# Moving two of VectorE's per-step products to GpSimd, and keeping the output chain in PSUM, in a scan kernel for eight cores

## The reference, cut to what matters

```python
xn = layernorm(x)
x_in, res = silu(xn @ Win[:D].T), xn @ Win[D:].T
dlt, B, C = split(x_in @ Wx.T)                      # 16, 1024 and 1024 wide
delta = clip(softplus(dlt @ Wdt.T + b), 1e-5, 0.1)
# for each token t, each of 1024 channels, each of 16 states:
dA = clip(exp(A * delta), 1e-6, 1)
h  = clip(h * dA + B * delta * x_in, -100, 100)
y  = sum(h over states) * C + Dp * x_in
out = x + (y * silu(res)) @ Wout.T + b_out + ffn(xn)
```

## Time and profile before

| | |
|---|---|
| time, median of 3 runs | 1364.24 us (1362.29 to 1365.52) |
| the profiled execution | 1363.85 us |
| its span on the slowest core (core 5) | 1362.3 us |
| DVE busy | 1329.3 us, 98% |
| ACT busy | 1190.7 us, 87% |
| PE busy | 1159.2 us, 85% |
| POOL busy | 72.0 us, 5% |

### The profile page before, as it was taken

How to read it: one execution, slowest core, us unless ns; L and a number is a source line. 1 busy time by engine, 2 the same in 40 slices (tenths; PEclk the granted TensorE clock), 3 DMA queues, 4 the chain that set the end, 5 groups by cost and what they waited for, 6 DMA issues and landing times.

```text
span 1362.3 us, 16727 instructions; the slowest of 8 cores (1356.8 to 1362.3 us)
## 1 busy us (share of the span) xinstructions
PE 1159.2 (85%) x4352; PEld 454.8 (33%) x4352; DVE 1329.3 (98%) x821; ACT 1190.7 (87%) x1899; POOL 72.0 (5%) x101
## 2 busy tenths in 40 slices
PE   5687886899888888799997898898888999878987
PEld 2232332333333333233333343333333333333432
DVE  6899999999999999999999999999999999999996
ACT  3899989989899898998989989899988988799781
POOL 1010100000000000000000000000000000110100
PEclk9886776878778898777778887788977888898877
DMA  9666855455654465444583555554554346454421
GB/s 278 100 110 98 126 99 141 108 109 89 117 117 72 109 124 98 104 111 86 117 127 72 102 116 126 80 108 92 106 101 90 54 78 139 82 147 85 93 50 63
DMA packets 94508, 143.97 MB, mean 106 GB/s; under 512 B 31232, under 2 KB 55360, under 8 KB 94416
## 3 DMA queue, kind: packets, MB, share of 16 engines
q1 hardware_dynamic: 80736, 117.99, 35.4%
q0 software_dynamic: 13680, 24.91, 17.4%
HBM read 101.45 MB, written 35.65 MB: 101 GB/s over the span
## 4 chain that ended last, share of the span: by engine, by line
PE 28%; DVE 28%; issue 21%; ACT 18%; DMA 4%; DVEq 1%; ACTq 0%; SPq 0%
DVE h L734 24%; ACT da L894 10%; PE pS L500 7%; PE pB L467 4%; DMA u<-u 3%; PE pC L477 3%; PE pX L435 2%; PE pO L435 2%; PE pR L487 2%; PE pO L514 2%; PE pO L511 2%; PE pX L511 2%; DVE y L750 1%; PE pX L514 1%; ACT L894 1%
## 5 line engine op out<-in xcount | busy, mean ns | idle before, releaser
L734 DVE TENSOR_TENSOR_SCAN h<-da,u 128x2056 f16<-128x2056 f16 x256 | 1119.5, 4424 | 3.4 <-ACT da L877 1.8
L894 ACT ACTIVATE da<-dl,consb 128x512 f16<-128x512 f16 x1024 | 651.7, 711 | 1.7 <-DVE dl L753 1.0
L500 PE MATMUL pS<-h,eye 128*128 128x512 f16 x1024 | 316.5, 442 | 160.3 <-DVE h L734 160.1
L500 PEld LDWEIGHTS pS<-h,eye 128*128 128x128 f16 x1024 | 102.2, 107 | 340.5 <-issue 316.0
L467 PE MATMUL pB<-xin,wx 128*128 128x512 f16 x512 | 167.9, 488 | 2.8 <-DMA wx<-w_x 2.2
L477 PE MATMUL pC<-xin,wx 128*128 128x512 f16 x512 | 140.8, 425 | 0.0
L487 PE MATMUL pR<-xnT,win 128*128 128x512 f16 x512 | 137.0, 417 | 0.0
L365 POOL DMA_DIRECT2D yt<-ost x56 | 47.8, 854 | 1049.1 <-ACT ost L955 1017.2
L467 PEld LDWEIGHTS pB<-xin,wx 128*128 128x128 f16 x512 | 54.3, 116 | 96.1 <-issue 87.2
L477 PEld LDWEIGHTS pC<-xin,wx 128*128 128x128 f16 x512 | 55.6, 109 | 79.1 <-issue 63.3
L894 ACT ACT_TABLE_LOAD x63 | 80.8, 1283 | 1.1
(11 more groups left out here) (140 smaller groups left out, 917.6 us busy)
## 6 DMA issues: line engine op xcount, KB each, us to landing
wo<-wos SPq DMA_DIRECT2D x56, 512.0 KB, 6.5
xt<-x SPq DMA_DIRECT2D x48, 512.0 KB, 5.9
u<-u SPq DMA_DIRECT2D x62, 384.0 KB, 3.2
yt<-xt SPq DMA_DIRECT2D x60, 256.0 KB, 7.8
yt<-ost POOLq DMA_DIRECT2D x56, 256.0 KB, 5.6
wx<-w_x POOLq DMA_DIRECT2D x15, 256.0 KB, 8.9
xnT<-x SPq DMA_DIRECT2D x4, 512.0 KB, 7.1
da<-w_in SPq DMA_DIRECT2D x4, 512.0 KB, 11.3
```

The lines of the kernel that those rows point to most:

```text
L500: mm = te.matmul(pS[s % 2][:, :], eye[:, :], h[:, n * SEG + 2:(n + 1) * SEG], start=(n == 0), stop=(n == NST - 1))
L734: v.tensor_tensor_scan(h[:, g * GW:(g + 1) * GW], da[:, g * GW:(g + 1) * GW], u[p][:, :], 0.0, op0=ALU.mult, op1=ALU.add).then_inc(v_scan, 1)
L894: sc.activation(da[:, n * SEG + 2:(n + 1) * SEG], dl[s % 2][:, :], AF.Exp, scale=cc(C_AL + k * NST + n)).then_inc(act_da, 1)
```

## The change

`t1` and `u` of steps 2 to 63 are computed on GpSimd, in a new function `dt_x(w)` that heads GpSimd's part of step s = w−1. It waits until DVE has finished scan(s,0). DVE keeps them only for steps 0 and 1. The tile `y1` goes: the three output operations work in place in the PSUM bank `pS[z % 2]` and follow one another on DVE with nothing between. clip_carry of groups 1 to 3 comes behind them. The clip of `dl` moves to the end of a step, behind scan(s,3), and serves step s+2. The waits named above go to the new producers: SP and ACT wait on `g_u` and `g_t1`, and PE waits for `v_y` in place of `v_SC`.

```diff
-        y1 = sb("y1", [128, TC], F32)
...
@@ SP
-                    sy.wait_ge(v_u, s + 2)
+                    sy.wait_ge(g_u, s)
                     sy.dma_start(... u[p] -> u[p] ...).then_inc(d_u[p], 16)
@@ GpSimd
+            def dt_x(w):
+                c, k = divmod(w, DCH)
+                gp.wait_ge(v_cl, w + 1)
+                gp.wait_ge(v_u, min(w, 2))
+                if w >= 3:
+                    gp.wait_ge(g_u, w - 2)
+                gp.wait_ge(v_scan, (w - 1) * NG + 1)
+                gp.tensor_tensor(t1[:, :], dl[w % 2][:, :], seg(xin[c % 2], k), op=ALU.mult).then_inc(g_t1, 1)
+                gp.wait_ge(g_t1, w - 1)
+                gp.wait_ge(act_B, w + 1)
+                gp.tensor_tensor(u[w % 2][:, 2:SEG], Bf[w % 2][:, :], t1[:, :], op=ALU.mult).then_inc(g_u, 1)
...
             for s in range(0, NSL):
+                if 2 <= s + 1 < NSL:
+                    dt_x(s + 1)
                 for (c, m) in out_at[s - 1]:
                     accumulate(c, m)
@@ PE
                 if g == 0 and s >= 2:
-                    te.wait_ge(v_SC, s - 1)
+                    te.wait_ge(v_y, s - 1)
@@ DVE
-                if 0 <= s - 1 and keeps(s - 1):
-                    clip_carry(s - 1, 1, NG)
...
-                    v.tensor_mul(y1[:, :], pS[z % 2][:, :], Cf[z % 2][:, :]).then_inc(v_SC, 1)
-                if w < NSL:
-                    (clip of dl[w % 2])
-                if 0 <= z < NSL:
+                    v.tensor_mul(pS[z % 2][:, :], pS[z % 2][:, :], Cf[z % 2][:, :]).then_inc(v_SC, 1)
                     v.wait_ge(v_SC, z + 1)
-                    v.scalar_tensor_tensor(y1[:, :], seg(xin[c % 2], k), cc(C_D + k), y1[:, :],
+                    v.scalar_tensor_tensor(pS[z % 2][:, :], seg(xin[c % 2], k), cc(C_D + k), pS[z % 2][:, :],
                                            op0=ALU.mult, op1=ALU.add).then_inc(v_D, 1)
-                    v.tensor_mul(t1[:, :], dl[w % 2][:, :], seg(xin[cw % 2], kw)).then_inc(v_t1, 1)
...
-                    v.tensor_mul(seg(yb[c % 2], k), y1[:, :], rs[z % 2][:, :]).then_inc(v_y, 1)
+                    v.tensor_mul(seg(yb[c % 2], k), pS[z % 2][:, :], rs[z % 2][:, :]).then_inc(v_y, 1)
-                        v.tensor_mul(u[w % 2][:, 2:SEG], Bf[w % 2][:, :], t1[:, :]).then_inc(v_u, 1)
+                if 0 <= s - 1 and keeps(s - 1):
+                    clip_carry(s - 1, 1, NG)
...
                     scan(s, 2)
                     scan(s, 3)
+                    if s + 2 < NSL:
+                        clip_dl(s + 2)
@@ ACT
-                    if w >= 2:
+                    if w >= 4:
+                        sc.wait_ge(g_t1, w - 3)
...
+                    if w >= 4:
+                        sc.wait_ge(g_u, w - 3)
```

More of the change, by code:

```diff
@@ L179, in build_core @@
         v_eye, v_ini, v_ac, v_bc = sem("v_eye"), sem("v_ini"), sem("v_ac"), sem("v_bc")
-        g_io = sem("g_io")
+        g_io, g_t1, g_u = sem("g_io"), sem("g_t1"), sem("g_u")
         d_cons, d_g = sem("d_cons"), sem("d_g")
@@ L554, in last_mm @@
                     else:
-                        te.wait_ge(v_SC, NSL - 7 + m)
+                        te.wait_ge(v_y, NSL - 7 + m)
                 for k in range(k0, k1):
@@ L735, in scan, with clip_dl @@
                                      0.0, op0=ALU.mult, op1=ALU.add).then_inc(v_scan, 1)
+            def clip_dl(w):
+                v.wait_ge(act_ln, w + 1)
+                v.tensor_scalar(dl[w % 2][:, :], dl[w % 2][:, :], 0.1, 1e-5,
+                                op0=ALU.min, op1=ALU.max).then_inc(v_cl, 1)
             for s in range(-1, NSL + 1):
@@ L749, in _ @@
                     v.wait_ge(act_C, z + 1)
-                    v.tensor_mul(y1[:, :], pS[z % 2][:, :], Cf[z % 2][:, :]).then_inc(v_SC, 1)
-                if w < NSL:
-                    v.wait_ge(act_ln, w + 1)
-                    v.tensor_scalar(dl[w % 2][:, :], dl[w % 2][:, :], 0.1, 1e-5,
-                                    op0=ALU.min, op1=ALU.max).then_inc(v_cl, 1)
-                if 0 <= z < NSL:
+                    v.tensor_mul(pS[z % 2][:, :], pS[z % 2][:, :], Cf[z % 2][:, :]).then_inc(v_SC, 1)
                     v.wait_ge(v_SC, z + 1)
-                    v.scalar_tensor_tensor(y1[:, :], seg(xin[c % 2], k), cc(C_D + k), y1[:, :],
+                    v.scalar_tensor_tensor(pS[z % 2][:, :], seg(xin[c % 2], k), cc(C_D + k), pS[z % 2][:, :],
                                            op0=ALU.mult, op1=ALU.add).then_inc(v_D, 1)
-                if w < NSL:
-                    cw, kw = divmod(w, DCH)
-                    v.wait_ge(v_cl, w + 1)
-                    v.tensor_mul(t1[:, :], dl[w % 2][:, :], seg(xin[cw % 2], kw)).then_inc(v_t1, 1)
-                if 0 <= z < NSL:
                     v.wait_ge(v_D, z + 1)
@@ L769, in _ @@
                         v.wait_ge(d_wff, 32)
-                    v.tensor_mul(seg(yb[c % 2], k), y1[:, :], rs[z % 2][:, :]).then_inc(v_y, 1)
-                if w < NSL:
+                    v.tensor_mul(seg(yb[c % 2], k), pS[z % 2][:, :], rs[z % 2][:, :]).then_inc(v_y, 1)
+                if 0 <= s - 1 and keeps(s - 1):
+                    clip_carry(s - 1, 1, NG)
+                if w < 2:
+                    clip_dl(w)
+                    v.wait_ge(v_cl, w + 1)
+                    v.tensor_mul(t1[:, :], dl[w][:, :], seg(xin[0], w)).then_inc(v_t1, 1)
                     v.wait_ge(v_t1, w + 1)
                     v.wait_ge(act_B, w + 1)
-                    if w >= 2:
-                        v.tensor_mul(u[w % 2][:, 2:SEG], Bf[w % 2][:, :], t1[:, :]).then_inc(v_u, 1)
[L776 to L779, removed]
+                    v.tensor_mul(bass.AP(u[w], 2, [[GW, 128], [SEG, GRP], [1, TC]]),
+                                 Bf[w][:, :].unsqueeze(1).broadcast_to([128, GRP, TC]),
+                                 t1[:, :].unsqueeze(1).broadcast_to([128, GRP, TC])).then_inc(v_u, 1)
                 if s == -1:
@@ L908, in _ @@
                     sc.wait_ge(act_e, w + 1)
-                    if w >= 2:
+                    if w >= 4:
+                        sc.wait_ge(g_t1, w - 3)
+                    elif w >= 2:
                         sc.wait_ge(v_t1, w - 1)
```

## The result

1375.95 us (median of 4 runs, 1375.69 to 1376.92) against 1364.86 us for the kernel before beside it: ratio 1.0089, 95% interval 1.0077 to 1.0101. The change makes the kernel slower by 0.9%. The forecast was 1383 with a range of 1355 to 1410.

What follows compares the result with a forecast made beforehand. The prediction took DVE to be full, with four fifths of its time in the 256 scans. DVE's own −2.8 us plus a 21.6 us hold by GpSimd made +18.8 us, so 1383 us, range 1355 to 1410.

Steps and rivals of the forecast that it cites:

- What leaves DVE's queue: DVE between y and scan(s,1): without t1, u and the clip of dl it loses 0.40 us in 62 steps, −24.8 us.
- What comes back: On DVE, the clip of dl ahead of the next scan, +12.4 us, and clip_carry behind yb with its wait, +9.6 us.
- DVE's own sum: What leaves and comes back on DVE, with no hold by GpSimd: −24.8 + 12.4 + 9.6 = −2.8 us.
- PSUM at nothing: Output chain in PSUM in place of SBUF: costed at nothing, bounds 6 us to either side.
- GpSimd's product, 1.16 us: Each 512-column product on GpSimd: 1.16 us, the middle of 0.63 and 1.69.
- The hold, 21.6 us: scan(s,1) waits for the rest of GpSimd's second product: 14 steps of 0.55 us and 48 of 0.29, 21.6 us.
- Late u, GpSimd's DMAs, SP's queue, PE's v_y at nothing: Later u and its copy, GpSimd's later accumulate, SP's shifted loads and PE's new wait: all costed at nothing.
- the 9 us of slack: How late u's copy may be before DVE waits at the scan that reads it: 9 us.
- the likeliest case: DVE's own sum plus the whole hold, +18.8 us: 1383 us, 1.4% slower, chance 0.52; its own range 1367 to 1410.

## Why the prediction was right

The sign, the size and the mechanism came out; the terms of the sum, one by one:

- *What leaves DVE's queue, −24.8 us.* y to scan(s,1) was 2.31 us without carry, as taken from step 63. Right, though the working beside it doesn't give it: 0.67 and 0.20 less the two gaps of 0.10 and 0.17 are 0.60, and the other 0.2 is that starts which had overlapped the end of the one ahead do so no longer. With carry the stretch loses 0.43 (2.74 less 2.31; there are six operations in it, not seven), 1.4 us more in 48 steps.
- *What comes back, +12.4 and +9.6.* The clip of dl costs 0.18 to 0.20 us ahead of scan(s,0). clip_carry with its wait cost 0.27 us where nothing held it (767.14 to 767.41 with half the columns), against 0.26. Right. DVE's own sum of −2.8 us was measured, with GpSimd's half columns, at −3.0 by the medians.
- *PSUM at nothing.* Right: ratio 1.0004 for that part alone. It was not nothing beside GpSimd, as the prediction also said: with the chain in SBUF the add and yb are held as well, 50 us.
- *GpSimd's product, 1.16 us.* 1.15. The bounds were 0.63 and 1.69, so that the middle came true is in part luck. The Trainium skill ("GPSIMD Engine Reference", section 3.1) gave an estimate of 1.12, and the trace agrees within 3%. The first start was 0.14 us behind the scan (752.64 to 752.78), not 0.30, and the second 0.21 us behind the first, not 0.15: the pair ends 2.65 us behind scan(s,0) by the records, 2.77 was forecast.
- *The hold, 21.6 us.* It was real: 0.28 us in nearly each of the steps, with carry (0.45 and 0.43 us of clip_carry in place of 0.15) and without (13.38 against 13.10 us), 62 × 0.28 = 17.4 us. Two things were off and half cancelled, so the size is in part luck. The hold ends 0.1 to 0.2 us before GpSimd's recorded end, so 0.55 in the steps without carry was too much (by half, with the pair done 0.12 us early). And in the carry steps I had only the scan down as held, at 0.29, where clip_carry came first and was held itself, by 0.28; by the prediction's own terms, with clip_carry due at 2.22 us, it would have been 0.55.
- *Late u, GpSimd's DMAs, SP's queue, PE's v_y at nothing.* No wait of the scans for them shows, 6.7 us of idle time ahead of 256 scans in all. The copy of u takes longer to land (6.6 us in the page's median, 3.2 before), well inside the 9 us of slack.

−2.8 + 17.4 = 14.6 us. From y to y the steps agree (20.49 us with carry, 752.56 to 773.05, against 20.21). The profiled spans differ by 13.0 us and the medians by 11.1, but the spans of the slowest cores are not a clean measure: core 7 of the changed kernel came to its first scan at 50.29 us, core 5 of the kernel before at 45.98, and over all cores and versions that start lies between 44.2 and 51.5. Counted from the first scan to the end of the span and averaged over the eight cores, the profiled executions are 1313.4 us before, 1325.8 changed, 1308.4 with half the columns and 1308.8 with the early start in the changed kernel. So the change costs 12.4 us; the hold is 17.0 to 17.4 of it, as summed, and DVE's own order gives back 4.6 to 5.0 rather than 2.8. Of the 2 us more, 1.6 lie at the end, where DVE waited 2.80 us for the last sums where it had waited 4.42.

The range has a fault that didn't show. By its own terms the likeliest case's ends, with start and product both short or both long, are 1364 and 1427 us, not 1367 and 1410.

The Trainium skill ("SBUF — State Buffer", section "SBUF: two separate sides") says that one port pair is locked for whole instructions, against DVE operations with two SBUF inputs or in a mode that uses both ports. The runs agree for the scan, and for the add and yb in SBUF, which are held, and for y, the add and yb with one input in PSUM, which are not (0.67, 0.75 and 0.69 us beside t1 and u). The clip with one input is held too; that would be the second clause, but no trace here shows the mode in which it ran. The runs part from the page in one point: a held instruction went on 0.1 to 0.2 us before the other's recorded end.

## What to carry to other kernels

When work goes to GpSimd beside a full VectorE, lay the two timelines on one another and ask of each VectorE instruction that falls into a GpSimd product whether it can be held; short clips can. Taking interleaved work away opens the waits that it covered: here 0.87 us a step, the two products and the clip of dl, was worth 0.40, and the clip took 0.20 back in its new place. A GpSimd product whose data are ready may be released one long VectorE instruction early: it is held through that and computes right at its end, which undid the whole hold here (17 us). But look at what VectorE does next: where that was the short clip, the same early start cost 30 us, and where VectorE had a gap ahead of the long instruction, the product went in first and held it in some steps. And a wait on one's own last instruction keeps the waits behind it from being taken early; put the others ahead of it.

## What the runs showed of the hardware that I had not expected

- A clip of 12 strided fp16 columns with one input was held by GpSimd's product, 0.45 us for 0.15, and 1.06 us in the worst order.
- A held instruction shows as longer, not as idle: t1 stood at 4.97 us of "busy" for some 1 us of work, and POOL's share with it.
- Five waits on one queue cost 0.21 us of idle time on DVE where they stood behind a wait on its own last scan, and none where they stood ahead of it; it was not late data, since only their place changed.
- Half the columns took GpSimd 0.66 us against 1.15; a line through the two, an estimate, is 1.9 ns a column and some 0.17 us fixed.
